# The mask of the diagonal maximum pieces moved from TensorE to VectorE, and one step of the denominator sums exchanged between TensorE and GpSimd

## What is computed

```python
k = (c_kv @ W_k_up).reshape(B, T, NH, HD); v = (c_kv @ W_v_up).reshape(B, T, NH, HD)
q = (x @ W_q).reshape(B, T, NH, HD)
scores = einsum('bqhd,bkhd->bhqk', q, k) + einsum('bqr,bkr->bqk', q_rope, k_rope)[:, None]
scores = scores / sqrt(HD + D_R)
scores = where(causal, -inf, scores)
w = softmax(scores, axis=-1)
attn = einsum('bhqk,bkhd->bqhd', w, v).reshape(B, T, D_MODEL)
```

## Time and profile before

| | before |
|---|---|
| median of 3 runs | 4143.91 us (4136.22 to 4147.65) |
| profiled execution | 4142.44 us, span 4140.7 us |
| PE busy | 3845.6 us, 93% of the span |
| DVE busy | 2803.9 us, 68% |
| POOL busy | 2441.1 us, 59% |
| ACT busy | 1795.5 us, 43% |
| granted TensorE clock | 0.959 of full speed |

### The profile page before, as it was taken

How to read it: one execution, slowest core, us unless ns; L and a number is a source line. 1 busy time by engine, 2 the same in 40 slices (tenths; PEclk the granted TensorE clock), 3 DMA queues, 4 the chain that set the end, 5 groups by cost and what they waited for, 6 DMA issues and landing times. The chain is left out here.

```text
span 4140.7 us, 58048 instructions
## 1 busy us (share of the span) xinstructions
PE 3845.6 (93%) x20832; PEld 2468.4 (60%) x20832; DVE 2803.9 (68%) x4366; ACT 1795.5 (43%) x3401; POOL 2441.1 (59%) x1149
## 2 busy tenths in 40 slices
PE   7999689999999999999999999999999599999998
PEld 4777455555555555555555555555555377777777
DVE  5777466767767677676676776667766277777776
ACT  2333234545445454455445445445445233333332
POOL 1333237667666676676766767667666455555555
PEclk9999789999999999999999999999999799999999
DMA  5888864353452634625336244353440211111110
GB/s 181 284 287 288 250 124 91 79 120 72 100 111 58 132 69 90 133 56 116 79 83 130 61 111 94 75 120 72 100 108 9 104 51 61 61 61 61 61 61 31
DMA packets 238409, 438.46 MB, mean 106 GB/s; under 512 B 25332, under 2 KB 26868, under 8 KB 238072
## 3 DMA queue, kind: packets, MB, share of 16 engines
q1 hardware_dynamic: 238136, 435.68, 40.8%
q10 hardware_dynamic: 64, 0.02, 0.0%
HBM read 300.86 MB, written 134.23 MB: 105 GB/s over the span
## 5 line engine op out<-in xcount | busy, mean ns | idle before, releaser
L835 DVE TENSOR_REDUCE att_piece_max<-att_ps_m 128x1 f32<-128x512 f32 (+3 forms) x2560 | 1484.4, 606 | 780.7 <-PE att_ps_m L940 452.7
L796 ACT ACTIVATE att_probs<-att_ps_s 128x512 f32<-128x512 f32 (+3 forms) x2560 | 1306.7, 534 | 1349.7 <-PE att_ps_s L957 1258.2
L904 POOL TENSOR_TENSOR att_sum_g<-att_sum_g,att_probs 128x2048 f32<-128x2048 f32 (+3 forms) x384 | 1442.0, 3755 | 186.8 <-ACT att_probs L796 156.3
L956 PE MATMUL att_ps_s<-att_q_a,att_k_a 128*128 128x512 f32 (+3 forms) x2560 | 1008.1, 398 | 21.8 <-DMA att_q_b<-att_neg_max 21.8
L957 PE MATMUL att_ps_s<-att_q_b,att_k_b 65*128 65x512 f32 (+3 forms) x2560 | 943.0, 373 | 0.0
L938 PE MATMUL att_ps_m<-att_k_a,att_q_a 128*128 128x512 f32 (+3 forms) x1840 | 700.6, 402 | 51.4 <-DMA att_q_a<-s_qr_hi 29.5
L963 PE MATMUL att_ps_o<-att_probs,att_v 128*32 128x512 f32 (+3 forms) x5120 | 607.2, 547 | 55.4 <-POOL att_probs L882 55.3
L956 PEld LDWEIGHTS att_ps_s<-att_q_a,att_k_a 128*128 128x128 f32 x2560 | 502.5, 196 | 147.2 <-issue 77.3
L938 PEld LDWEIGHTS att_ps_m<-att_k_a,att_q_a 128*128 128x128 f32 x1840 | 352.7, 196 | 390.5 <-DVE att_piece_max L835 214.2
L957 PEld LDWEIGHTS att_ps_s<-att_q_b,att_k_b 65*128 65x128 f32 x2560 | 495.4, 194 | 64.7
L901 POOL TENSOR_TENSOR att_sum_g<-att_probs 128x2048 f32<-128x2048 f32 x48 | 220.0, 4583 | 336.1 <-PE att_ps_d L963 197.8
(11 more groups left out here) (176 smaller groups left out, 5202.8 us busy)
## 6 DMA issues: line engine op xcount, KB each, us to landing
att_q_a<-s_q_hi SPq DMA_DIRECT2D x128, 256.0 KB, 5.2
att_q_a<-s_qr_hi SPq DMA_DIRECT2D x128, 256.0 KB, 6.0
prj_x_sb<-in_x_dram SPq DMA_DIRECT2D x16, 1024.0 KB, 5.4
s_q_hi<-prj_q_hi SPq DMA_DIRECT2D x16, 1024.0 KB, 4.4
s_q_lo<-prj_q_lo SPq DMA_DIRECT2D x16, 1024.0 KB, 6.4
s_k_hi<-prj_k_hi SPq DMA_DIRECT2D x16, 1024.0 KB, 6.8
s_k_lo<-prj_k_lo SPq DMA_DIRECT2D x16, 1024.0 KB, 7.8
s_v<-prj_v_sb SPq DMA_DIRECT2D x16, 1024.0 KB, 8.7
```

The costliest lines, as they stand in the source:

```text
L796: act.activation(probs[s % RING][:, hh, c0:CH], ps_s[(GH * s + hh) % SBANKS][:, c0:CH], ACT.Exp, scale=SCALE).then_inc(probs_ready, 1)
L835: dve.tensor_reduce(piece_max[:, j, hh * TB + r, kc:kc + 1], ps_m[:, bank, 0:width], AX_X, ALU.max).then_inc(piece_taken, 1)
L904: pool.tensor_tensor(sum_g[:, :, c0:CH], sum_g[:, :, c0:CH], new, ALU.add).then_inc(sum_added, 1)
L956: mm(out[:, c0:CH], k_a[:, hh, i * P:(i + 1) * P], q_a[j][:, hh, c0:CH], start=True, stop=False)
```

## The change

The mask matmul goes. The diagonal piece is now one matmul of its width, and DVE reads it with a `tensor_tensor_reduce` that adds a float32 mask of 128 x 512 from SBUF (zeros, with the triangle in its last 128 columns, of which the last `width` columns are read), writes the sum back to the piece's PSUM bank and keeps the maximum. Pieces off the diagonal are reduced as before. In SHARE_OF, blocks 1 to 3 have their last T before the diagonal moved to the first diagonal step. That step, and the one where the T was, are both 512 columns wide. Set-up makes one float32 mask and one identity in place of four tiles.

```diff
-SHARE_OF = ("TTTT", "GGGTGGGG", "GGGTGGGTGGGG", "GGGTGGGTGGGTGGGG")
+SHARE_OF = ("TTTT", "GGGGTGGG", "GGGTGGGGTGGG", "GGGTGGGTGGGGTGGG")
...
-                    width = CH if kc < j else (r + 1) * P
-                    dve.tensor_reduce(piece_max[:, j, hh * TB + r, kc:kc + 1], ps_m[:, bank, 0:width], AX_X,
-                                      ALU.max).then_inc(piece_taken, 1)
+                    top = piece_max[:, j, hh * TB + r, kc:kc + 1]
+                    if kc < j:
+                        dve.tensor_reduce(top, ps_m[:, bank, :], AX_X, ALU.max).then_inc(piece_taken, 1)
+                    else:
+                        width = (r + 1) * P
+                        dve.tensor_tensor_reduce(ps_m[:, bank, 0:width], ps_m[:, bank, 0:width], keep["mask_qk"][:, CH - width:CH],
+                                                 1.0, MASKED, ALU.add, ALU.max, top).then_inc(piece_taken, 1)
...
-                last = mm(ps_m[:, bank, 0:width], q_a[j][:, hh, r * P:(r + 1) * P], keys, start=True, stop=(kc < j))
-                if kc == j:
-                    last = mm(ps_m[:, bank, width - P:width], keep["ident_b"][:], keep["mask_qk"][:], start=False, stop=True)
-                last.then_inc(piece_ready, 1)
+                mm(ps_m[:, bank, 0:width], q_a[j][:, hh, r * P:(r + 1) * P], keys, start=True, stop=True).then_inc(piece_ready, 1)
...
-            "ident_f": sb("ident_f", [P, P], F32), "ident_b": sb("ident_b", [P, P], BF16),
-            "mask_kq": sb("mask_kq", [P, P], BF16), "mask_qk": sb("mask_qk", [P, P], BF16),
+            "ident_f": sb("ident_f", [P, P], F32),
+            "mask_qk": sb("mask_qk", [P, CH], F32),
```

More of the change, by code:

```diff
@@ L18 @@
 F32R = mybir.dt.float32r
-BF16 = mybir.dt.bfloat16
 ALU = mybir.AluOpType
@@ L108, in _ @@
             pool.memset(keep["ident_f"][:], 0.0).then_inc(fill, 1)
-            pool.memset(keep["ident_b"][:], 0.0).then_inc(fill, 1)
-            pool.memset(keep["mask_kq"][:], 0.0).then_inc(fill, 1)
             pool.memset(keep["mask_qk"][:], 0.0).then_inc(fill, 1)
[L112 to L120, removed]
+            pool.wait_ge(fill, 2)
+            pool.affine_select(out=keep["ident_f"][:], in_=keep["ident_f"][:], compare_op=ALU.not_equal, fill=1.0,
+                               base=0, pattern=[[-1, P]], channel_multiplier=1).then_inc(filled, 1)
+            pool.affine_select(out=keep["mask_qk"][:, CH - P:CH], in_=keep["mask_qk"][:, CH - P:CH], compare_op=ALU.is_ge, fill=MASKED,
                                base=0, pattern=[[-1, P]], channel_multiplier=1).then_inc(filled, 1)
@@ L172, in _ @@
                 mm.then_inc(row_ready, 1)
-            pe.wait_ge(filled, 4)
+            pe.wait_ge(filled, 2)
             for i in range(4):
```

## The result

The changed kernel takes 4081.9 us (median; 4078.2 to 4085.9) against 4145.8 us: ratio 0.9836, 95% interval 0.9817 to 0.9856. Forecast were 4036 us with a range of 3990 to 4095. The direction and the range hold; of the forecast gain of 107 us, 64 arrived. The profiled execution has a span of 4076.5 us (before 4140.7): attention, taken from the first to the last score matmul, went from 2721.7 to 2662.4 us, and the few us left are spread over the other two stages.

What follows compares the result with a forecast made beforehand. PE was taken to set the pace. Savings of 7.2 us a unit gave 101 us over fourteen units, plus 10 for first and last, less 1.6: 109, rounded to 107; forecast 4036 us, range 3990 to 4095.

Steps and rivals of the forecast that it cites:

- part 1: PE without the mask matmul: 0.10 us saved a diagonal piece, 6.4 us a unit if PE could use all.
- steps 19 to 21: Stretch of 16 diagonal pieces where DVE has room: the whole 1.6 us of saved mask time stays.
- e: DVE's extra time for each masked diagonal piece, taken as 0.1 us, between 0 and 0.45.
- part 2: DVE's new add-and-maximum instruction: its extra time per piece, and whether DVE has room for it in each stretch.
- a rival with a chance of 0.17: DVE's maximum costs a second, accumulator-reading instruction: extra time about 0.25 us a piece, about 4060 us; chance 0.17.
- The rival that is locked out by POOL: DVE's new instruction waits for the end of POOL's additions: +47 us a unit, about 4890 us; chance 0.04.
- Steps 5 to 12: Block 1: 0.5 us of mask time kept in steps 5 to 8, 0.7 from PE's vanished wait for POOL.
- Steps 23 to 28: Block 2's end and after: 0.9 us of mask time kept, plus 0.9 from PE's vanished wait for POOL's clearing.
- The end of block 3: POOL's 4.58 us addition made one step sooner shortens its closing chain: 2.6 us a unit, 1.6 of masks included.
- The first and the last unit: Gain of 5 us each, less than a middle unit: own loads disturb one, the other has only 32 diagonal pieces.
- this collision: Block 1: POOL's additions follow directly where `o_sb` waits; DVE isn't held for a second one, POOL loses 0.25 us.
- The clock: Low granted clock at the unit's end may go with PE's waits: up to 2.7 us a unit, about 3995 us.

Runs made afterwards that it cites:

- the mask alone: Kernel before with the mask moved from PE to VectorE and the old SHARE_OF: 4153.8 us, ratio 1.0026.
- the unmasked version: Changed kernel with block 1's maxima transfer issued early and no mask on the diagonal pieces, reduced by plain tensor_reduce: 4055.1 us, ratio 0.9759.
- masked twin: Changed kernel, mask kept on VectorE, with block 1's maxima transfer issued ahead of block 3's query loads and output store: 4015.5 us, ratio 0.9685.
- the fillers: Useless 128x256 matmuls where PE waits for POOL: on the unmasked version 4011.5 us; on the mask alone, also in steps 23 and 24, 4111.2 us.

## Why the prediction was right in sign and short in size

- *The mask's price on PE* (part 1, 0.10 us a piece) holds: steps 19 to 21 took 12.6 us where 14.1 - 1.6 = 12.5 were forecast.
- *e* (part 2) was taken as 0.1 and is 0.16 us: 0.02 for the main instruction, where the 691 ns row had given 0.005, and 0.14 for the accumulator's read, which I had made a rival with a chance of 0.17: that rival's instruction came true inside a forecast that had left it out. By the Trainium skill, "VectorE: DVE Perf Modes" (section "Two Vector instructions with no wait between them"), such an operation is two instructions; the trace agrees. But the rival's price was wrong too (e of 0.25, and 4060 us). Leaving e out gives 0.24 us a unit in steps 8 and 9, and doubling it costs 0.17 there. VectorE had the room.
- *The rival that is locked out by POOL* didn't occur: in a stretch in which POOL adds without a break the new instruction takes 0.68 to 0.73 us at 512 columns. The prediction says of the Trainium skill, "SBUF — State Buffer" (section "Who interferes with whom"), that it doesn't tell whether the new instruction takes the shared ports. It does tell: a VectorE instruction with at most one input in SBUF, outside the two-port modes, doesn't contend with GpSimd; the trace agrees.
- *Steps 5 to 12* were forecast at 0.5 + 0.7 = 1.2 us a unit and gave 0.9 in the mean of units 1 to 14. `o_sb` ended 0.55 us behind POOL's addition as before, PE ran into the three banks behind it (0.61 us of idle time), and the wait of 0.66 us for POOL went.
- *Steps 23 to 28* were forecast at 0.9 for the masks and 0.9 for the wait that goes. By the means of units 1 to 14 they gave 1.0 in all (25.9 to 24.9 us). The wait behind `o_sb` in step 28 grew from 1.13 to 1.81 us, since the work ahead of it had become shorter and POOL's addition had not: 6.8 us became 7.0. In six of the 16 units the clock fell behind this wait, and the step took 8.5 to 8.7 us. In block 3's start 0.53 us went to a second transfer of maxima that is now just late.
- *The end of block 3* was forecast at 2.6 us and gave 3.3 in the mean of units 1 to 14. Part of it is the clock: the time at its lower level in steps 35 to the end fell from 79 to 17 us, and the forecast had counted no such relief. POOL's rows there: second clearing at 1696.12, last addition ending at 1704.02 + 1.26 = 1705.28, 9.2 us as forecast (9.1), against the earlier trace rows.

```profile
1696.12 0.63 POOL L879 TENSOR_SCALAR_AFFINE_SELECT att_probs<-att_probs 128x512 f32<-128x512 f32 x1 [0.39 <-ACT att_probs L789]
...
1704.02 1.26 POOL L901 TENSOR_TENSOR att_sum_g<-att_sum_g,att_probs 128x512 f32<-128x512 f32 x1
```

- *The first and the last unit* were forecast at 5 us each and became 0.2 and 1.3 us longer, 11.5 us of what was missing. Both lose by the exchanged step: the first unit's step 8 went from 7.1 to 11.7 us (6.8 with the mask alone), the last unit's last four steps from 13.7 to 18.3 (14.9 with the mask alone). In the first unit's step 8 `o_sb` came 0.2 us after POOL's second addition had begun, was held for all of it (4.84 us), and PE waited 4.37 us for DVE. In the last unit POOL runs behind PE, so that one more addition ahead of the first clearing makes PE wait:

```profile
571.05 4.84 DVE L845 TENSOR_TENSOR att_o_sb<-att_o_raw,att_rden 128x512 f32<-128x512 f32 x1
...
3174.03 1.93 PE L957 MATMUL att_ps_o<-att_probs,att_v 128*32 128x512 f32 x8 [6.03 <-POOL att_probs L879]
```

The prediction had settled this collision from the one row in which `o_sb` gets in between the earlier trace rows.
- *The largest failure is in the sum*, not in a term of it. It took what is saved at a unit's end as saved for good, and never asked what else is timed from there. The next unit's loads start with the last scores, take their time whatever PE does, and block 1's maxima queue behind them. Before, the maxima landed 1.7 us ahead of PE (the median of units 1 to 15; 0.8 in unit 6), now PE is ready 2.0 us ahead of them, and with the slow clock behind it an idle time that grew by 24 us cost 42.5, where the forecast was short of 43 (107 - 64). With that one transfer moved, the same change gives 4015.5 us. That the two amounts agree so closely is luck. A unit of the middle fourteen gained 4.4 us instead of 7.2: 3.1 went back in steps 3 and 4 and steps 5 to 28 fell short by 1.1, while steps 0 to 2 (0.7, not forecast) and the unit's end (0.7 more than forecast) made up for some of it, both places where the clock was better; the first and last unit fell short by 11.5 in all, and the two other stages gave 4.9, which the forecast didn't have.
- *The clock* was in the prediction as a chance on the good side. It is more than that: it took about 44 us from the mask alone, about 31 from the unmasked version and nearly half of what the late maxima cost.

**What stays open:** why the clock falls at the unit's end in the unmasked version and not in its masked twin, with PE waits of 0.85 and 0.79 us. The runs show that keeping PE fed settles it, not what decides between the two. The kernel before was not tried with the fillers, so what the change is worth at a held clock isn't known. The two parts were not tried one by one with both the early transfer and the fillers.

## What to carry to other kernels

When a change shortens a stretch, list the transfers that are issued from its end and compare their landing with their use before summing: a small transfer behind large loads has their latency, and its margin belongs in the sum. Issue the small, urgent one first; here that was worth 1.5% after the change and 0.15% before it. And where the bottleneck engine waits on another one, work removed from it turns into a longer wait and, on TensorE, possibly into a lower clock: look at the granted clock around each wait before counting removed matmuls as time.

## What the runs showed of the hardware that I had not expected

- VectorE's addition with maximum in one operation (one input in PSUM, one in SBUF, written back to PSUM) takes 707 ns at 512 columns, 21 ns more than the plain reduction, and a separate read of the accumulator of 141 ns. It isn't held up by GpSimd's additions: in block 1 of unit 6 its 384 and 512 wide instances take 0.54 to 0.59 and 0.68 to 0.73 us while POOL adds without a break.

```profile
1567.30 0.54 DVE L832 CUSTOM_DVE_ANT_0 att_ps_m<-att_ps_m,mask_qk 128x384 f32<-128x384 f32 x1
...
1574.65 0.73 DVE L832 CUSTOM_DVE_ANT_0 att_ps_m<-att_ps_m,mask_qk 128x512 f32<-128x512 f32 x1
```

- Less work for VectorE made a kernel slower (ratio 0.9759 against 0.9685, intervals 0.9716 to 0.9801 and 0.9659 to 0.971). In the traces it shows as the same matmuls at the lower clock, and two useless matmuls a unit took it back.
